# One core, 32 sequences: a new hand-written order of work on all four engines, with reordered waits

## The reference, cut to what matters

```python
x = x + s6(layernorm(x)); x = x + moe(layernorm(x))
# s6, 256 hidden channels, 16 states each
u, o = x @ W_in.T;  u = silu(causal_conv4(u) + conv_b);  g = u @ W_gate.T
delta = softplus(g[:64] @ W_delta.T + delta_bias);  b, c = g[64:80], g[80:96]
h_t = exp(A * delta_t) * h_{t-1} + (delta_t * u_t) * b_t     # over time
y = sum_states(h_t * c_t) + D * u;  y = y * silu(o);  return y @ W_out.T
# moe: 8 experts of width 176, top 2 by softmax, weights scaled by 2.5, and a shared part of width 352
w = top2(softmax(x @ gate_w.T)) * 2.5
y = sum_e w_e * (silu(x @ w_gate_e) * (x @ w_up_e)) @ w_down_e + shared(x)
```

## Time and profile before

| | before |
|---|---|
| median of three runs | 1346.92 us (1346.78 to 1347.88) |
| profiled execution, its own time | 1347.99 us |
| its span, first to last instruction | 1346.3 us |
| mean granted TensorE clock | 0.958 of full speed |
| busy: PE, DVE, ACT, POOL | 1160.7, 1126.5, 1044.9, 1142.5 us |
| HBM read, written | 41.04 MB, 5.24 MB |

### The profile page before, as it was taken

How to read it: one execution, slowest core, us unless ns; L and a number is a source line. 1 busy time by engine, 2 the same in 40 slices (tenths; PEclk the granted TensorE clock), 3 DMA queues, 4 the chain that set the end, 5 groups by cost and what they waited for, 6 DMA issues and landing times. The chain is left out here.

```text
span 1346.3 us, 26240 instructions
## 1 busy us (share of the span) xinstructions
PE 1160.7 (86%) x9075; PEld 930.5 (69%) x9075; DVE 1126.5 (84%) x1762; ACT 1044.9 (78%) x2155; POOL 1142.5 (85%) x536
## 2 busy tenths in 40 slices
PE   3455999999999989999999999999999999998787
PEld 2323777777777777777777777777777777776677
DVE  3466799999998999899988989989889998898853
ACT  3877788888888788888887888888888888887742
POOL 3299799999999999999999999999999999999820
PEclk8767899999999999999999999999999999998899
DMA  4343323434343224443332333333432334333000
GB/s 109 108 101 88 85 72 86 100 100 104 73 103 97 74 77 100 103 100 81 95 103 70 79 99 100 100 87 90 103 81 74 93 100 100 91 78 98 5 5 9
DMA packets 71486, 115.09 MB, mean 85 GB/s; under 512 B 8173, under 2 KB 30394, under 8 KB 71354
## 3 DMA queue, kind: packets, MB, share of 16 engines
q1 hardware_dynamic: 67178, 110.71, 32.4%
q10 hardware_dynamic: 4176, 2.70, 0.7%
HBM read 41.04 MB, written 5.24 MB: 34 GB/s over the span
## 5 line engine op out<-in xcount | busy, mean ns | idle before, releaser
L405 POOL TENSOR_TENSOR inject<-rep,bc 128x1024 f32<-128x1024 f32 x256 | 604.1, 2384 | 10.7 <-DMA rep<-dd 9.9
L414 POOL TENSOR_TENSOR read<-state,bc 128x1024 f32<-128x1024 f32 x224 | 529.1, 2377 | 35.7 <-DVE state L689 28.1
L689 DVE TENSOR_TENSOR_SCAN state<-decay_ps,inject 128x1024 f32<-128x1024 f32 x224 | 508.3, 2281 | 27.7 <-ACT decay_ps L483 25.3
L483 ACT ACTIVATE decay_ps<-rep,neg_a 128x255 f32<-128x255 f32 x1024 | 423.1, 460 | 27.1 <-DVE state L689 24.8
L923 PE MATMUL work_ps<-xn2T_part,ffn_gate 128*128 128x256 f32 x1344 | 218.7, 300 | 46.2 <-ACT g_silu L471 39.4
L471 ACT ACTIVATE g_silu<-work_ps 128x512 f32<-128x512 f32 x224 | 134.5, 601 | 133.1 <-PE work_ps L923 111.6
L923 PEld LDWEIGHTS work_ps<-xn2T_part,ffn_gate 128*128 128x128 f32 x1344 | 182.0, 195 | 77.8 <-ACT g_silu L471 55.0
L957 PE MATMUL acc_ps<-ffn_down,features 128*128 128x128 f32 (+1 forms) x1792 | 229.0, 277 | 0.0
L957 PEld LDWEIGHTS acc_ps<-ffn_down,features 128*128 128x128 f32 (+1 forms) x1792 | 213.0, 191 | 4.5
L707 DVE TENSOR_TENSOR features<-g_silu,work_ps 128x512 f32<-128x512 f32 x224 | 152.2, 680 | 75.2 <-ACT g_silu L471 40.1
L932 PE MATMUL work_ps<-xn2T_part,ffn_up 128*128 128x256 f32 x1344 | 197.6, 287 | 0.0
(11 more groups left out here) (138 smaller groups left out, 1394.4 us busy)
## 6 DMA issues: line engine op xcount, KB each, us to landing
rep<-dd SPq DMA_DIRECT2D x256, 256.0 KB, 4.7
bc<-bc_rows SPq DMA_DIRECT2D x64, 512.0 KB, 4.8
x_in<-in_L_attn_x_dram SPq DMA_DIRECT2D x32, 128.0 KB, 2.1
out_dram<-result SPq DMA_DIRECT2D x32, 128.0 KB, 1.8
bc_rows<-g_sb SPq DMA_DIRECT2D x32, 32.0 KB
state<-in_L_ffn_w_gate_dram ACTq DMA_DIRECT2D x1, 704.0 KB, 4.4
read<-in_L_ffn_w_up_dram ACTq DMA_DIRECT2D x1, 704.0 KB, 5.9
ffn_down<-in_L_ffn_w_down_dram ACTq DMA_DIRECT2D x1, 704.0 KB, 6.9
```

Of the source, the lines that this page charges most:

```text
L405: pool.tensor_tensor(inject[:, at % RI], du_all, b_all, ALU.mult).then_inc(inject_done, 1)
L414: pool.tensor_tensor(read[:, at % RR], state[:, at % RS], c_all, ALU.mult).then_inc(read_done, 1)
L483: last = act.activation(decay_ps[:, at % 2, j, 1:T], rep[(HALVES * n + half) % RP][:, j, 0, 1:T], ACT.Exp, scale=neg_a[:, col:col + 1])
L689: dve.tensor_tensor_scan(to, decays, inject[:, at % RI].rearrange("p j t -> p (j t)"), 0.0, ALU.mult, ALU.add).then_inc(state_done, 1)
```

## The change

The arithmetic, the tiles, the buffers and the transfers stay as they are, and SP's list is the same. What changes is the order of instructions in the other four lists, and where some waits stand:

* **POOL**: `read_group(0)` moves ahead of `inject_group` 2 and 3, and `read_group(5)` ahead of `inject_group(k+1, 0)`. Waits that repeat an earlier one of the same half are dropped.
* **ACT**: silu 1 and 2 stand before `xn`. The high copy of xnT stands between decays 2 and 3, `expd` after decays 3, the rest copy before decays 4. `combT` and `log_var` stand after the table change that follows decays 4, and before the logarithm. `neg_mean` stands after decays 5. Abs, exp and the addition of one stand together, and `rstd` behind them. Decays (k+1, 0) stand behind both copies of xn2T. The two large copies of the expert weights (k = -1 only) stand behind u.
* **DVE**: scan 0 opens the step, before pair 0; the first norm's statistics (`bn_stats`, `bn_aggr`) stand behind `take_y(k-1, 1)`, between scans 0 and 1; `result` stands after scan 1, x1 before scan 2, the chain of the expert weights and the second norm's statistics between scans 2 and 3; pair 4 ahead of `read_own_group`; weigh 0 ahead of `take_y(k, 0)`; weigh 2 ahead of scan 5; weigh 4 and `z_less` ahead of scan 6.
* **PE**: in full below as far as it can be cut. The sums over states 7, 0, 1, 3, 5, 6 stand elsewhere among the experts' matmuls, `gates(4)` stands ahead of the convolution, `spread_comb` 2 and 4 stand earlier, down 11 to 13 ahead of `ups(3)`, down 9 ahead of L1130, and down 10 ahead of sum 6.

```diff
 POOL
-                    pool.wait_ge(rep_in[half], 16 * JB * (n + 1))
-                    pool.wait_ge(b_in, 16 * (n + 1))
+                    if g == 0:
+                        pool.wait_ge(rep_in[half], 16 * JB * (n + 1))
+                        if half == 0:
+                            pool.wait_ge(b_in, 16 * (n + 1))
...
                 injects(1)
+                reads(0)
                 injects(2)
                 injects(3)
-                reads(0)
                 reads(1)
...
+                reads(5)
                 if on(1):
                     inject_group(k + 1, 0)
-                reads(5)
 ACT
...
                 if on(0):
                     decays(k, 2)
-                    decays(k, 3)
                 if on(2):
                     n = k + 2
                     act.wait_ge(xnT_mm, n + 1)
                     act.wait_ge(gate_mm, n)
                     act.copy(xnT_parts[0][:, TAPS - 1:], xnT_ps).then_inc(xnT_high, 1)
+                if on(0):
+                    decays(k, 3)
+                if on(-2):
+                    act.wait_ge(shifted_done, f + 1)
+                    act.activation(expd[:], shifted[:], ACT.Exp).then_inc(expd_done, 1)
...
+                if on(0):
+                    decays(k, 4)
+                if on(3) or on(-1) or on(1):
+                    act.preload_act_table_set("natural_log")
                 if on(-2):
                     act.wait_ge(combT_mm, f + 1)
                     act.wait_ge(cb_mm, COMBS * f)
                     act.copy(combT[:], combT_ps).then_inc(combT_done, 1)
-                if on(0):
-                    decays(k, 4)
-                if on(3) or on(-1) or on(1):
-                    act.preload_act_table_set("natural_log")
...
                     act.activation(z_e[:], z_ps, ACT.Abs).then_inc(z_abs_done, 1)
+                    act.wait_ge(z_abs_done, n + 1)
+                    act.activation(z_e[:], z_e[:], ACT.Exp, scale=-1.0).then_inc(z_exp_done, 1)
+                    act.wait_ge(z_exp_done, n + 1)
...
+                    act.activation(z_w[:], z_e[:], ACT.Identity, bias=1.0).then_inc(z_one_done, 1)
                 if on(3) or on(-1):
                     act.wait_ge(ln_small, 2 * (k + 4))
                     act.activation(rstd[:], log_var[:], ACT.Exp, scale=-0.5).then_inc(ln_rstd, 1)
...
-                if on(1):
-                    decays(k + 1, 0)
...
                     act.copy(xn2T_parts[n % 2][1][:], xn2T_ps).then_inc(xn2T_low, 1)
                 if on(1):
+                    decays(k + 1, 0)
                     decays(k + 1, 1)
 DVE
...
+                    dve.wait_ge(ffu_mm, at + 1)
                     dve.wait_ge(silu_done, at + 1)
-                    dve.wait_ge(ffu_mm, at + 1)
                     dve.wait_ge(down_mm, count(CHUNKS * (f - 1) + 2 * p + 2))
...
+                if on(0):
+                    scan(0)
+                pairs(0)
+                if on(-1):
+                    take_y(k - 1, 1)
                 if on(3):
...
 PE
...
                     gates(1, f)
+                if on(-1):
+                    sum_states(k - 1, GROUPS - 1)
+                if on(-2):
                     pe.wait_ge(silu_done, pair(0))
                     ups(1, f)
...
+                if on(-2):
+                    if on(-1):
+                        pe.wait_ge(x1_done, k)
+                    else:
+                        pe.wait_ge(silu_done, pair(3))
+                    gates(4, f)
+                if on(0):
+                    sum_states(k, 1)
                 if on(-2):
                     pe.wait_ge(comb_split, 2 * f + 2)
...
                     pe.wait_ge(hc_done, COMBS * f + 2)
                     spread_comb(3)
+                    pe.wait_ge(hc_done, COMBS * f + 3)
+                    spread_comb(4)
...
                     down(7, f)
-                    pe.wait_ge(hc_done, COMBS * f + 3)
-                    spread_comb(4)
-                if on(0):
-                    sum_states(k, 5)
...
                 if on(-2):
                     down(8, f)
+                    down(9, f)
...
                     pe.matmul(xn2T_ps, neg_identr[:], xn2T_parts[n % 2][0][:], start=False, stop=True,
                               skip_group_check=True).then_inc(xn2T_rest, 1)
-                if on(-2):
-                    down(9, f)
+                if on(0):
+                    sum_states(k, 5)
```

More of the change, by code:

```diff
@@ L490, in body @@
                     silu(0)
+                    silu(1)
+                    silu(2)
                 if on(2):
@@ L572, in body @@
                     last.then_inc(u_done, 1)
+                if on(1) and not on(0):
+                    act.wait_ge(ffn_loaded, 16 * len(ffn_loads))
+                    act.wait_ge(padded, 2)
+                    act.copy(ffn_gate[0][:], gate_staged).then_inc(ffn_high, 1)
+                    act.copy(ffn_up[0][:], up_staged).then_inc(ffn_high, 1)
                 if on(-2):
@@ L815, in body @@
                     scan(4)
[L816 removed]
+                pairs(4)
                 if on(1) and not on(0):
@@ L822, in body @@
                                       ALU.subtract).then_inc(ffn_ready, 1)
-                pairs(4)
+                if on(0):
+                    read_own_group()
                 pairs(5)
                 pairs(6)
+                if on(-2):
+                    weigh(0)
                 if on(0):
@@ L842, in body @@
                     weigh(3)
-                if on(0):
-                    scan(6)
+                    weigh(4)
                 if on(2):
@@ L852, in body @@
                 if on(0):
+                    scan(6)
                     scan(7)
                 if on(-2):
-                    weigh(4)
                     weigh(5)
@@ L1039, in body @@
                     last.then_inc(conv_mm, 1)
-                if on(-2):
-                    if on(-1):
-                        pe.wait_ge(x1_done, k)
-                    else:
-                        pe.wait_ge(silu_done, pair(3))
-                    gates(4, f)
                 if on(0):
@@ L1075, in body @@
                     ups(6, f)
+                    pe.wait_ge(silu_done, pair(6))
+                    spread_comb(0)
                 if on(0):
@@ L1152, in body @@
                     gates(0, n)
+                if on(-2):
+                    down(10, f)
                 if on(0):
```

129 lines of the change are left out of this document (51 added, 78 removed).

## The result

The changed kernel takes 1282.88 us (median of 4 runs, 1281.89 to 1283.93), the kernel before 1346.99 us beside it (4 runs, 1346.78 to 1347.88). The ratio is 0.952, with a 95% interval of 0.951 to 0.954.

The account below looks back on a forecast made before the run. A loop through ACT, then PE, was taken to bound each step. 28 x (38.29 - 36.80) = 41.7, ramp 2.0, steps 30 and 31 2.0, tail 0.7: 46.4 gained, 1300.5 us against the median; range 1283 to 1326.

Parts of the forecast that it names:

- The loop of two halves: Steady step: ACT from gate of o to silu 4, 12.34, then PE to the next gate, 25.92; together 38.26.
- Half A: ACT from the gate of o to the end of silu 4: 12.34 less a wait of 0.47, giving 11.87.
- the walk: One new step traced with the profile's durations: `gates(5)` at 12.0, the next gate at 36.65.
- a bound of 0.3: Dropped and exchanged waits, costed at nothing; at most three of seven pairs on the loop, 0.1 each per step.
- half B: PE from `gates(5)` to the next gate of o: waits of 0.66 and 0.33 go, 25.92 becomes 24.93.
- 36.80: Predicted steady step by PE and ACT alone, 11.87 + 24.93, in us; 38.29 before, over 28 steps.
- rival 2: Steady step shorter: DVE's remaining waits go too, 0.7 a step, giving 36.1 and 1281 us; chance 16%.
- The second term: Ramp: two ACT copies moved behind u bring the first inject from 60.10 to 58.1, 2.0 gained.
- The end: Steps 30 and 31 gain 1.0 each; the tail gains 1.28 and 0.7, loses 1.3, net 0.7.
- 1: Rival: rstd holds POOL and POOL holds the sums over states; step 37.6, 1323 us; chance 20%.
- 4: Rival: no change, the new waits fall where the old ones were; chance 3%.
- Rival 3: Scan 0 late on DVE, decays behind the xn2T copies; at 3.2 late step 38.7, 1353 us; chance 7%.

Follow-up runs that it names:

- the pad on POOL: The changed kernel with one thrown-away product of 384 columns on POOL ahead of each shift; ratio 0.955 to the kernel before, step 36.27.
- the pad on PE: The changed kernel with the two matmuls of spread_comb(5) computed twice on PE; ratio 0.957 to the kernel before, step 36.38.

## Why the prediction was right or wrong

Right were the direction and the mechanism:

* The loop of two halves. After the change they sum to the step again, 12.02 + 24.24 = 36.26. Half A, predicted as 11.87 and 12.0 by the walk, was 12.02.
* The waits at L1122 and L1130 are gone; a wait of 0.15 before `gates(5)`; POOL's wait for rstd is 0.98 (1.1 predicted) and off the loop, as the pad on POOL shows. The wait before the transpose of the expert weights is 0.17 and not 0.8, because sum 1 ahead of it waits 1.15 for its product from POOL, which the prediction did not have; half A runs through ACT and did not feel it.
* Scan 0 ahead of pair 0 costs nothing: silu 0 is late anyway. The prediction stopped at "nothing"; taking the new head of DVE's list out costs 1.4 a step.
* The waits: 0.1 a step against a value of nothing and a bound of 0.3.

The step that failed is "25.92 - 0.99 = 24.93", half B on PE. The halves and places were right; the term was mis-sized. Measured: 24.24. The half lost 1.68 where 0.99 was predicted, and the missing 0.69 has two parts. The two waits cost 1.26 from start to next start, so to take the wait printed at a matmul as its whole cost left out 0.27. The other 0.42 is in no wait: the prediction had "the same matmuls as before" cost the same in new places, and they cost less, 0.27 among the transposes and down products and 0.15 from the pair of combine matmuls, less what stands behind the logits. That is the bookkeeping of two traces; no run put z_less back behind scan 6 in the changed kernel. With half A 0.15 longer than 11.87 the step is 0.5 shorter than 36.80, 14 of the 18 us. Taken as itself, 36.26 lies just below the forecast's own 36.4 to 37.2, and a touch above rival 2's 36.1: rival 2 gave nearly the right number by luck, as far as the runs tell. It let DVE's small waits go and priced a loop through DVE; what the rows show is half B on PE. That DVE is not the loop is argued (it is busy 34.61 of the step), and no run tested it.

The second term is the ramp, by 3.8 us. Of its own argument the logarithm came at 47.10, as forecast (49.67 - 2.6), and rstd held the first inject, as forecast. That inject starts at 59.63 after 60.10 in the two profiled executions, 0.5 earlier instead of 2.0, as the four matmuls of z, which rstd stands behind, took 2.07 at a granted clock of 0.50. In four of the experiments with the same list up to there (POOL's old order, sum 5, the pad on PE, DVE's old head) z takes 1.13 at a clock of 1.00 and the inject starts at 58.09 to 58.25, the forecast's 58.1; in the kernel before with only scan 0 moved it is 59.97. So the 2.0 is 1.7 to 1.9 where the clock is up over z and 0.5 where it is not.

The larger part is step 2, which the prediction priced like any other. In the profiled executions it was 4.8 longer than the steady 38.28 before and is 0.8 longer than 36.28 after. Of the 4.0 that went, 2.1 was the low clock in the one execution of before. Of the other 1.9 the xnT copies alone bring 1.2 (40.90 - 38.27 = 2.6 against 39.27 - 37.91 = 1.4). The places of sum 5 and of POOL's products act there too: undone in the changed kernel, they bring 1.9 and 0.8 back. These parts overlap, and they were not taken apart further.

The end brought 4.2 instead of 2.7: steps 30 to 32 gave 4.4 and the tail after the last shift -0.2, so the 1.28 and 0.7 for the tail did show up, but inside step 32, or not at all; this was not taken apart.

The Trainium skill's page "SBUF — State Buffer", section "SBUF: two separate sides", would have made the ramp's gain from the copies nothing. In the changed kernel's own trace the two subtractions on DVE (54.99 and 56.94, 2.02 each) were over at 58.96, before POOL's shift at 59.48, so it shows nothing of this. In the four experiments with the early inject the second subtraction overlaps the shift. POOL's timeline of the one with the pad on PE, whose second subtraction runs from 56.06 to 58.08:

```profile
57.84 0.29 POOL L442 TENSOR_TENSOR shift<-neg_mean,rstd 128x4 f32<-128x4 f32 x1 [18.28 <-ACT rstd L606]
```

In all four the shift takes 0.28 or 0.29, where it takes 0.20 in the steady step, and ends 0.05 or 0.06 behind the subtraction. That fits the page's rule and does not show it, since in the ramp shifts beside other DVE operations take 0.23 to 0.27 too. What it cost here is 0.1 us at most; POOL arrived only at the subtraction's end, so a whole subtraction of waiting was not put to the test.

The Trainium skill's page "ScalarE: Activation LUTs", section "What ACT_TABLE_LOAD costs", has a drain behind each load: after as before there is none in the trace (617.63 + 1.28, next operation at 618.93).

Of the rivals, 1 and 4 did not come in the steady step. Rival 3 did not come either. Its mechanism, everything behind the copies hanging on PE, is seen in small with sum 5 put back: copies 0.6 later, decays and silu 0 later, 0.55 a step, but scan 0 does not wait there. The experiment with z_less early shows the reverse order, decays that hold the copies, at 0.6 a step and with it a clock that falls in most steps. That the whole change avoids both because copies, decays, scan 0 and sum 5 were moved together is a reading of these runs and was not tested part by part.

## What to carry to other kernels

Price a wait on PE from the start of the group before it to its own start, less what that group takes undisturbed; the waits printed at the matmuls were 0.99 where these were 1.26. And do not take a group's cost with it to its new place: another 0.42 came from there. In a pipeline whose four engines are each 90% full, parts of a reordering can't be judged alone: here scan 0 ahead of pair 0 was worth nothing alone, while the list's head that it belongs to was worth 1.4 us a step in place, and two other parts made the kernel slower. And a share of the chain that ended last is no proof of a bound: a pad of a microsecond on the engine that it names settles it. Last, compare ramps between several executions: here a low clock in the one profiled execution of before made 2.1 us of what looked like the gain of one step.

## What the runs showed of the hardware

* Behind a wait PE's clock can fall, but does not each time. Behind the same wait of 2.42 to 2.43 us in step 2 the convolution took 5.09 and 5.17 in two kernels (granted clock 0.54 over six microseconds in one) and 3.13 in two others. Behind 1.64 to 1.9 the clock fell in five of 27 steps, with 1.1 to 1.7 at another place in seventeen of 27. In the changed kernel, with waits of 1.14 to 1.36 in every step, the windows view has 1.00 from 136 to 1160 us.
* Groups of matmuls cost by neighbour: four transposes 0.55 us from start to next start behind a wait, 0.45 behind down products; a repeated pair of combine matmuls 0.23 where the first of its kind took 0.43.
* 384 separate waits fewer, over all engines, with the swapped pairs were worth 0.1 us of a step of 36.3.
